# Four-layer attention and expert kernel: group 0's score maxima placed ahead of batch 1's chain in the two self-attentions, their transfers issued by ScalarE

## What is computed

```python
x = x + _L0_xattn_ref(_layernorm(x), ctx_1024, mask, Wq, Wk, Wv, Wo)   # 16 heads of 8, 77 keys
x = x + _L0_ffn_ref(_layernorm(x), ...)
...
def _L0_ffn_ref(...):                       # B, S, D, H = 2, 512, 128, 16 here; HEAD = 8
    resid = hidden_states
    x = layer_norm(hidden_states, ln1_w, ln1_b)
    q = (x @ q_w + q_b) / math.sqrt(HEAD); k = x @ k_w + k_b; v = x @ v_w + v_b
    scores = einsum('bhqd,bhkd->bhqk', q, k)
    scores = where(causal, scores, neg)     # layer 2 has no causal mask
    attn = softmax(scores)
    ctx = einsum('bhqk,bhkd->bhqd', attn, v)
    hidden = resid + (ctx @ o_w + o_b)
    ...                                     # then router, top-2 of 16 experts
```

## Time and profile before

| | us |
|---|---|
| median of 3 runs | 1214.75 (1213.97 to 1216.38) |
| the profiled execution's own time | 1213.29 |
| its span, first to last instruction | 1211.2 |
| TensorE busy in the span | 950.1 (78%) |
| VectorE, ScalarE, POOL busy | 561.1, 440.2, 242.0 |
| mean granted TensorE clock | 0.882 of full speed |
| self-attention u=0, from its first scores to its last turned values | 109 to 233 |
| self-attention u=1, the same | 718 to 855 |

### The profile page before, as it was taken

One profiled execution on the slowest core, in us unless ns is written; L12 is line 12 of the kernel. 1 busy time (PEld: TensorE's weight loads), 2 busy tenths in 40 slices (PEclk: granted clock), 3 DMA queues, 4 the chain that ended last, 5 costly groups with the idle time before them and its releaser, 6 DMA issues. The chain is left out here.

```text
span 1211.2 us, 15544 instructions
## 1 busy us (share of the span) xinstructions
PE 950.1 (78%) x5561; PEld 648.8 (54%) x5561; DVE 561.1 (46%) x1292; ACT 440.2 (36%) x769; POOL 242.0 (20%) x283
## 2 busy tenths in 40 slices
PE   5886789634737539999768757998699979869998
PEld 3564345324635335777637742232366677747776
DVE  4784456341237363111666846774254546631111
ACT  2332355412323113343353323776322233424443
POOL 0435211032053100000374343001000012430110
PEclk9998699956978759999797976999799988978999
DMA  7005210103620000110000052210010101200111
GB/s 321 1 1 141 92 47 22 36 18 104 184 74 1 1 0 18 36 35 18 1 1 1 2 122 87 55 27 2 1 38 29 58 14 59 70 1 18 35 35 36
DMA packets 33263, 55.71 MB, mean 46 GB/s; under 512 B 3696, under 2 KB 25397, under 8 KB 32816
## 3 DMA queue, kind: packets, MB, share of 16 engines
q1 hardware_dynamic: 32176, 52.88, 14.3%
q0 software_dynamic: 1024, 1.98, 0.6%
HBM read 44.81 MB, written 9.96 MB: 45 GB/s over the span
## 5 line engine op out<-in xcount | busy, mean ns | idle before, releaser
L2269 PE MATMUL psum<-xT_all,wexp 128*128 128x512 f32 x400 | 184.0, 605 | 1.3 <-issue 0.7
L1483 DVE TENSOR_REDUCE arena<-psum 128x2 f32<-128x1024 f32 (+3 forms) x128 | 127.7, 1021 | 71.5 <-PE psum L2057 43.5
L1038 ACT ACTIVATE arena<-psum 128x512 f32<-128x512 f32 (+3 forms) x256 | 115.9, 515 | 78.3 <-PE psum L2070 40.1
L732 POOL TENSOR_TENSOR rstd<-var,held 128x4 f32<-128x4 f32 (+3 forms) x30 | 54.4, 1826 | 403.0 <-DVE var L1241 385.9
L2269 PEld LDWEIGHTS psum<-xT_all,wexp 128*128 128x128 f32 x400 | 74.4, 196 | 78.3 <-issue 72.6
L1975 PE MATMUL psum<-values_out_all,arena 128*128 128x128 f32 x560 | 80.5, 294 | 35.6 <-ACT arena L1005 26.3
L2284 PEld LDWEIGHTS psum<-wexp,arena 128*128 128x128 f32 x800 | 94.2, 192 | 16.1 <-issue 14.3
L2054 PE MATMUL psum<-arena 72*128 72x512 bf16 (+3 forms) x256 | 80.1, 384 | 27.2 <-DVE arena L1483 12.9
L798 POOL TENSOR_TENSOR arena<-arena,small 128x616 f32<-128x616 f32 x56 | 67.9, 1216 | 147.0 <-DVE small L1424 146.9
L2284 PE MATMUL psum<-wexp,arena 128*128 128x128 f32 x800 | 94.7, 275 | 0.9 <-DVE r_res L1746 0.9
L1975 PEld LDWEIGHTS psum<-values_out_all,arena 128*128 128x128 f32 x560 | 71.1, 202 | 43.7 <-ACT arena L1005 33.6
(11 more groups left out here) (282 smaller groups left out, 1439.3 us busy)
## 6 DMA issues: line engine op xcount, KB each, us to landing
wexp<-experts SPq DMA_DIRECT2D x32, 514.0 KB, 3.5
parts_k<-wexp SPq DMA_DIRECT2D x12, 384.0 KB, 2.8
arena<-parts_k SPq DMA_DIRECT2D x48, 96.0 KB
arena<-parts_q SPq DMA_DIRECT2D x48, 96.0 KB
arena<-experts SPq DMA_DIRECT2D x8, 514.0 KB, 3.8
wexp<-experts SPq DMA_DIRECT2D x9, 384.0 KB, 3.1
held<-packed SPq DMA_DIRECT2D x1, 2375.0 KB, 15.3
held<-packed SPq DMA_DIRECT2D x1, 2264.5 KB, 20.4
```

The source lines that it names most:

```text
L732: pool.tensor_tensor(dst, src, half[0:src.shape[0], 0:n], ALU.pow).then_inc(done, 1)
L1038: act.activation(p_self[:, n % 2, kt % 2, j, lo:S], bank(t_bank("keys", c, k), lo, S), ACT.Exp, scale=DS ** -0.5).then_inc(ut_ok, 1)
L1483: dve.tensor_reduce(top[:, x % 2, qt, j:j + 2], src, AX_X, ALU.max, negate=True).then_inc(us_ok, 1)
L2269: mm(bank(c, 0, BANK), wexp[:, side, c * P:(c + 1) * P], xT_all[:, b * S:(b + 1) * S], start=True, stop=True).then_inc(h_ps, 1)
```

## The change

1. **Layer 0's preparation.** The context keys and values go to PSUM banks 7 and 6 (before 0 and 3). The key entries of TensorE wait for their own batch's multiply (`k_own`, b+1) and no longer for the values; VectorE does `own_values` right behind `own_keys`, ahead of the scaling of x.
2. **Memset of ones** (POOL, L783 before, L798 now): from ahead of the pipeline into it, before half 6, in layers 0 and 2. `pads_ok`'s memset no longer has it ahead.
3. **Batch 1's chain.** On VectorE `self_moments`, `self_residual`, `self_normal` stand behind maximum(7), (9) and (11). On TensorE and ScalarE the turn stands at tick 1, keys and queries at tick 2, the values at tick 3, in the same rotating PSUM places as the rest. On POOL group 0's maxima come ahead of all of batch 1's work, and batch 1's split behind group 1's maxima. On SP batch 1's store and the expert loads stand behind what belongs to group 0.
4. **The maxima's transfers** are issued by ScalarE: behind its copy L1058 (L1045 before) it waits for that copy and issues four (L1061), ahead of the tick's exponentials (L1051). SP's `load_top` is gone.

```diff
@@ sync
-            def load_top(u, x):
-                sp.wait_ge(ut_ok, t_count(u, "top", x))
-                for j in range(4):
-                    sp.dma_start(q_ring[ROWS:ROWS + 3, x % 4, j, :], top_row[3 * j:3 * j + 3, x % 2, :]).then_inc(top_in[x % 2], 16)
...
                 for x in range(4):
                     load_group(u, x)
-                store_split(u, 1)
-                split_stored(sp, u, 1)
-                for side in range(2):
...
                 for x in range(GROUPS):
-                    load_top(u, x)
+                    if x == 1:
+                        store_split(u, 1)
+                        split_stored(sp, u, 1)
                     if 1 <= x < 5:
                         load_group(u, x + 3)
+                    if x == 1:
+                        for side in range(2):
...
@@ gpsimd
-                    pool.wait_ge(x_xTp, 2 * l + 2)
...
-                    pool.memset(U["k"][64:96, :], ONES_IN_PAIRS).then_inc(ones_set, 1)
-                    pool.wait_ge(ones_set, u + 1)
...
+                    if u is not None and n == 6:
+                        pool.wait_ge(e_mul, at)
+                        pool.memset(U["k"][64:96, :], ONES_IN_PAIRS).then_inc(ones_set, 1)
+                        pool.wait_ge(ones_set, u + 1)
...
-                batch_tokens(1, a_stat, SELF_AT[l] + 2, a_rstd)
-                batch_tokens(1, b_stat, B * u + 2, b_rstd)
-                pool.wait_ge(pT_ps, FIRST_HALF[l] + HALVES[l])
-                pool.memset(U["v1"], 1.0).then_inc(wide_set, 1)
-                split_keys(u, 1)
-                split_queries(u, 1)
...
                     pool.tensor_copy(parts[:, :, :, 2], top_rest).then_inc(top_ok, 1)
+                    if x == 0:
+                        batch_tokens(1, a_stat, SELF_AT[l] + 2, a_rstd)
+                        batch_tokens(1, b_stat, B * u + 2, b_rstd)
+                        pool.wait_ge(pT_ps, FIRST_HALF[l] + HALVES[l])
+                        pool.memset(U["v1"], 1.0).then_inc(wide_set, 1)
+                    if x == 1:
+                        split_keys(u, 1)
+                        split_queries(u, 1)
@@ scalar, top_out(x), ahead of the tick's exponent calls
                     act.activation(top_row[0:12, x % 2, :], bank(t_bank("top", x), 0, BANK, 12), ACT.Copy).then_inc(ut_ok, 1)
+                    act.wait_ge(ut_ok, t_count(u, "top", x))
+                    for j in range(4):
+                        act.dma_start(q_ring[ROWS:ROWS + 3, x % 4, j, :], top_row[3 * j:3 * j + 3, x % 2, :])\
+                           .then_inc(top_in[x % 2], 16)
@@ vector
-                self_moments(u, 1)
-                self_residual(u, 1)
-                self_normal(u, 1)
...
+                    if a == 7:
+                        self_moments(u, 1)
+                    if a == 9:
+                        self_residual(u, 1)
+                    if a == 11:
+                        self_normal(u, 1)
+                    if own_at(tick, "v"):
+                        self_values(u, 1, s_bank("own", "v"))
@@ tensor, prep
-                    pe.wait_ge(k_own, l + 1)
+                    if l:
+                        pe.wait_ge(k_own, l + 2)
                     for b, half in parts:
-                        if entry == 1:
+                        if l == 0:
+                            pe.wait_ge(k_own, b + 1)
+                        elif entry == 1:
                             pe.wait_ge(v_own, l + 1)
@@ tensor, selfattn
-                    if tick == 3 - LEAD:
-                        self_turned(u, 1, 4)
-                    if tick == 4 - LEAD:
-                        self_projected(u, 1, 0, 5)
-                        self_projected(u, 1, 1, 6)
-                    if tick == 5 - LEAD:
-                        self_projected(u, 1, 2, 4)
-                    if tick == 8 - LEAD:
-                        pe.wait_ge(hi_ok, 2 * B * (u + 1))
-                        pe.wait_ge(v_in_ok, B * (u + 1))
...
+                    if own_at(tick, "tokens"):
+                        t_free("own", "tokens")
+                        self_turned(u, 1, t_bank("own", "tokens"))
...
+def own_at(tick, *what):
+    return tick == {"tokens": 1, "k": 2, "q": 2, "v": 3}[what[0]]
```

More of the change, by code:

```diff
@@ L484, in program @@
                 s_place["router", routed_at(tick_)] = len(s_place)
+            for what_ in ("tokens", "k", "q"):
+                if own_at(tick_, what_):
+                    t_place["own", what_] = len(t_place)
+            if own_at(tick_, "v"):
+                s_place["own", "v"] = len(s_place)
         def s_count(u, *what):
@@ L1083, in selfattn @@
                         tokens_out(b)
+                    if own_at(tick, "tokens"):
+                        self_tokens(u, 1, t_bank("own", "tokens"))
+                    if own_at(tick, "k"):
+                        self_projected(u, 1, 0, t_bank("own", "k"))
+                    if own_at(tick, "q"):
+                        self_projected(u, 1, 1, t_bank("own", "q"))
             def moe_input(l):
@@ L1460, in self_values @@
                 dve.wait_ge(wide_set, B * u + b + 1)
-                dve.wait_ge(pj_ps, 3 * (B * u + b) + 3)
+                if b == 0:
+                    dve.wait_ge(pj_ps, 3 * u + 3)
+                else:
+                    dve.wait_ge(us_ps, s_count(u, "own", "v"))
+                done = v_in_ok if b == 0 else us_ok
                 dst = v_wide[b][:, :, :, 0:DS]
@@ L2018, in self_turned @@
                 pe.wait_ge(b_xn, B * u + b + 1)
-                turn_tiles(n, xn_self, 0, s_xTp)
+                turn_tiles(n, xn_self, 0, s_xTp if b == 0 else ut_ps)
             def self_projected(u, b, which, n):
-                pe.wait_ge(s_xT, 4 * u + b + 1)
+                if b == 0:
+                    pe.wait_ge(s_xT, 3 * u + 1)
+                else:
+                    pe.wait_ge(ut_ok, t_count(u, "own", "tokens"))
+                done = pj_ps if b == 0 else ut_ps if which < 2 else us_ps
                 wn = w(f"s{2 * u}_{'kqv'[which]}_w")
@@ L2029, in self_projected @@
                         last = mm(bank(n, t * P, (t + 1) * P), xT_self[:, t * P:(t + 1) * P], wn, start=True, stop=True)
-                last.then_inc(pj_ps, 1)
+                last.then_inc(done, 1)
             def selfattn(u):
@@ L2176, in selfattn @@
                         router(b)
+                    if own_at(tick, "tokens"):
+                        t_free("own", "tokens")
+                        self_turned(u, 1, t_bank("own", "tokens"))
+                    for which, what in enumerate("kq"):
+                        if own_at(tick, what):
+                            t_free("own", what)
+                            self_projected(u, 1, which, t_bank("own", what))
+                    if own_at(tick, "v"):
+                        s_free("own", "v")
+                        self_projected(u, 1, 2, s_bank("own", "v"))
             def project(first, src, weights):
```

87 lines of the change are left out of this document (48 added, 39 removed).

## The result

The changed kernel takes 1228.45 us in the median of six runs (1222.58 to 1245.97), the kernel before beside it 1214.36 us. The ratio is 1.0099, with an interval of 1.0077 to 1.0122: **slower by 1.0%, some 12 us**, outside the range of the forecast. The profiled execution of the changed kernel is the slowest of its six, 1245.97 us with a span of 1244.0, so it shows the loss larger than the median does.

What follows compares the result with a forecast made beforehand. One chain of stages, with hand-over waits at three starts and TensorE setting the steady pace: -7.0 - 3.0 - 7.6 + 18.3 = +0.7 us on 1213.29, plus 1.46 to the runs' median, gives 1215.4 us; range 1203 to 1224.

Steps and rivals of the forecast that it cites:

- Part 1, preparation: Layer 0's preparation: key entries start earlier and the first maximum no longer waits for the memset; 7.0 us gained, between 5.0 and 8.
- Part 2, the memset of ones: POOL's 3.50 us memset costs nothing in its new place; with thinner cover up to 2 us in each of two places.
- Part 3, batch 1's chain: Starts of both self-attentions: 7.6 us gained in u=0 and 3.0 us in u=1.
- Rival C: Clock does not rise in ticks 1 to 3 of the self-attentions: 7 us less gained, 1222; chance 0.13.
- The forecast's aside: By the skill's rule, moving the issues is neither gain nor loss and the sum would be 17.6 us faster.
- Part 4, the transfers on ScalarE: Both self-attentions: four issues delay the tick's exponentials, TensorE waits; 1.5 us a group in u=0, 1.25 in u=1, 18.3 us lost.
- B: Tick of each group's turn: issues hurt more, 0.83 us each, 7 us more lost, 1222; chance 0.10.
- A: An issue on ScalarE is cheap or its cost hidden: 4 us lost in place of 18.3, 1201; chance 0.17.
- D: The steady part absorbs more: half the loss of u=0 goes, 1211; chance 0.15.
- the signs that I had listed: First maximum near 28.3, POOL 8 to 9 us behind first scores, full clock from tick 3, ScalarE issues of 0.64 us.
- The period of about 14.4 us: u=1's group period grows from 13.1 to about 14.4 us, with TensorE waiting 1.2 to 1.6 us once a group.
- The rule of the Trainium skill: Issuing on several engines saves only sequencer time, usually small; the prediction held 0.64 us an issue against "small".

Runs made afterwards that it cites:

- e3: The kernel before with parts 1 and 2 of the change alone; 1207.87 us, ratio 0.9929.
- e5: As e1, SP's list reordered: group 2's transfers between batch 1's stores and the wait for them, two experts' loads at group 5; 1195.64 us, ratio 0.9832.
- e1: The changed kernel with SP issuing the four transfers of each group's maxima again, parts 1 to 3 kept; 1204.36 us, ratio 0.9882.
- e6: The changed kernel, four issues on ScalarE, with only the two experts' loads moved to group 5; 1230.64 us, ratio 1.0108.
- e7: As e5, with five unread copies on ScalarE behind each group's copy of the maxima, transfers still on SP; 1225.35 us, ratio 1.0102.
- e9: As e6, with seven useless extra products of the first turned block on TensorE in the tick behind each group's turn; 1217.45 us, ratio 1.0025.
- e10: As e5, with two of each group's four transfers issued by ScalarE and two by SP; 1195.43 us, ratio 0.9880.
- e8: As e6, with ScalarE's four issues parted: two, an exponential, two, the other exponential; 1223.06 us, ratio 1.0073.

## Why the prediction was wrong

**Part 1, preparation**: forecast -7.0, measured -8.6 with part 2 (e3; -6.6 to -10.6 by its interval). Right: the first maximum at 28.80 against "near 28.3".

**Part 2, the memset of ones**: forecast 0. No wait for it appears in the changed kernel; it is not measured apart.

**Part 3, batch 1's chain**: forecast -10.6, of it -7.6 in u=0. e5 against e3, part 3 with SP's order mended and SP's issues: 1195.64 - 1207.87 = -12.2. From first scores to the last copy, u=0 takes 204.10 - 102.32 = 101.8 us in e5 against 109.4 in e3: 7.6 us less, the forecast's number. In u=1 the start gained more than the 3.0 forecast: group 2's copy comes 48.0 us behind the first scores before and 43.6 in e5 (745.86 - 702.30), 4.4 us less. Rival C is refuted: the clock rose in batch 1's projections in both self-attentions. One thing my walk left out: with the chain moved, batch 1's stores, group 4's loads and the experts' loads fall among the first groups, and SP's list then delays group 2's transfers (e1). The forecast's aside that the kernel would be 17.6 us faster without part 4 holds with SP's order mended (e5: -20 by the ratio), not as the code stands (e1: -14).

**Part 4, the transfers on ScalarE**: forecast +18.3, measured 33 to 35 (e6 over e5). This is the step that failed. Its price for an issue (0.64, measured 0.68), its place (the tick of the turn), who waits (TensorE, 1.6 to 2.0 us on the exponential's line against 1.2 to 1.6) and its cost per group were right where the clock held: 1.25 in u=1 against 1.23 (e7) to 1.33 (e6, e9), 1.5 in u=0 against 1.07 to 1.46. With the clock nearly held (e9) the four issues cost 21.8 us in all, 3.5 more than the sum. What it lacked is a term: the loss of part 4 was walked in the steady part at the full clock throughout, because the rows of before had it there, so a fall of the clock behind the new waits was put at nothing, and no row was given for that. In the changed kernel the clock does fall there, to 0.83 and 0.79 in the two stretches, and e9 shows that 10 to 13 us of the cost are the clock's. With the gains (8.6 and 12.2 in place of 7.0 and 10.6) the sum becomes +12 to +14 us, and +12 was measured in place of +0.7. The gains' surplus of 3.2 us and the 3.5 us of blocking more than forecast cancel each other, which is luck.

**The rivals.** B had the right sign and the right place, at 1222, but by dearer issues (0.83 each), which they are not. A is refuted for four issues, though for two it is what happens (e10). D is refuted: u=0 absorbed at most 0.4 us in one group (13.34 against 12.27). Of the signs that I had listed most came out. The period of about 14.4 us did not: only the groups with a full clock have it (e6, e7, e9). TensorE's waits are longer than the 1.2 to 1.6 us named, and in u=1 POOL begins on group 0's maxima 10.6 us behind the first scores, as my walk had it (10.9), and not 8 to 9, as the sign said. I had named a low clock only as a danger in ticks 1 to 8, before the kernel had reached its pace.

The rule of the Trainium skill that the prediction weighed ("DMA: Bandwidth & Descriptors", section "Issuing engines are not separate DMA queues": sequencer time is usually small) does not hold for these transfers: four issues took 3.41 us from 113.59, and TensorE had the data at 118.11, 1.1 us behind the end of the last issue. At 0.68 us each, with eight groups of four in each self-attention, that is not small.

## What to carry to other kernels

A few instructions' worth of time on an engine that feeds the bound one can be free, and the next one dear: ScalarE's slack here was at least 1.4 us a group (an estimate: two issues of 0.68 us cost nothing in the period), so ask of a moved issue not its price alone but whether the slack of the tick where it stands is used up. When a change brings a new repeated wait into a stretch where TensorE ran at the full clock, price the stretch at the low clock too, and read the granted clock and the count of matmuls next to the busy time. And if a list of transfers on one queue is too long for a small urgent one, try the list's order first: moving one call and two loads (e5) removed the wait of 7.92 us and gained 6 to 9 us over e1, while moving the transfers to another engine removed the same wait and lost more than it gave.

## What was not expected of the hardware

In a steady part where TensorE is busy nine tenths of the time, a single wait of 1.65 us was followed by some 14 us at 1.2 GHz, and not in every group: with the same waits the clock fell in some groups and held in others, and e6's runs spread from 1215.88 us (clock 0.884 over the run) to 1242.68 (0.856). With waits for the exponentials of 0.7 us at most it held nearly throughout (e10: 0.96 over 160 to 200 and 0.99 over 760 to 840). A wait of over a microsecond is not enough by itself: in u=0 TensorE waits 1.11 us for POOL once in each group, in the kernel before too, and from 160 to 200 the clock there is 1.00. Adding 14 times seven useless matmuls made a kernel 10 to 13 us faster. The Trainium skill, "TensorE: Matmul & The Clock Gate", section "A second HAM failure mode: psum-queue depth-cycling", tells of a kernel whose frequent short idle spells between groups of matmuls made the clock swing between its levels; the changed kernel's trace agrees, with 0.83 and 0.79 in the two stretches above. Which wait sets off a fall and which does not stays open: in u=1 e8, with two waits of at most 0.6 us each in a group, had as low a clock as e6 with its single ones of 1.6 to 1.7 (0.83 in both), and in u=0, with waits of 0.9 and 1.11 us in each group, it held 1.00. So it is shown that ScalarE's extra time lowers TensorE's clock here, and that work in TensorE's wait brings it back; by what pattern of waits is not.
